# Splitting the last of seven rounds into two in a six-sum graph kernel

## The chip, the cores and the metric

One core of a Trainium2 chip runs the whole program. The metric is the device time of one execution in microseconds (us). The kernel before was timed three times: median 6155.66 us, from 6149.27 to 6156.11.

## The reference, cut to what matters

Four graph blocks work on 6250 nodes with 128 features and 100,000 edges whose destinations are sorted. Each block's result is added to its input and layer-normalised.

```python
edge_index = jnp.stack([src, dst])
x = _layernorm(x + _L0_gnn_ref(x, edge_index, ...))   # attention, 8 heads, then selu
x = _layernorm(x + _L1_gnn_ref(x, edge_index, ...))   # three times: x + segment_sum(x[src], dst), two dense layers
x = _layernorm(x + _L2_gnn_ref(x, edge_index, ...))   # attention, 4 heads, plus a skip product, its own norm
x = _layernorm(x + _L3_gnn_ref(x, edge_index, edge_weight, ...))  # three times: x @ W, weighted segment_sum, bias
```

The second and the fourth block each hold three sums over edges: these are the six sums of the title.

## The kernel before, in words

**Sums as matrix products.** The nodes are cut into 49 tiles of 128. The edges are scattered into two dense adjacency planes in device memory, one of edge counts (fp16) and one of edge weights (fp32). A sum over edges is then a dense product of the node rows with the plane. It is done in rounds of destination tiles, `ROUNDS = (7, 7, 7, 7, 7, 7, 7)` (L46). A round has 49 steps, one for each source tile: a strip of the plane (128 source nodes by 896 destination columns, and 128 extra columns in round 0) is brought by SyncE's DMA queue, and TensorE multiplies the source rows by it in one piece of 512 columns and one of 384, accumulating in two PSUM banks. After the 49 steps a small product (`fix`, L1050) adds a correction, the banks are drained, and the dense layers of the round (the "net") are run in pieces, one piece after every fifth step of the next round (L1133, and L1672 for the other engines). A round's tiles are cut into quads of at most four tiles (`quads_of`, L898), so a round has one quad of four and one of three.

**Three count sums** (`CountSums`, L1256; the order of work of each engine is written out in `count_layers`, L1693). The first ("alone") multiplies bf16 row parts with fp16 strips directly. Its rounds wait until GpSimd has scattered the cells that they read (`s_epoch`, L1361). The second ("wide", 256 features) needs, for each step: the fp16 strip widened to fp32r ("laid", L1426) into one of four strip buffers; a high part of the source rows made by ScalarE (`make_high`, L1437) and a low part made by VectorE (`make_low`, L1445), in a ring of two; then 8 matmuls of TensorE. `make_high` of step n waits for the matmuls of step n-2. The third has its high and low parts at hand, needs only the laid strip, and has 4 matmuls a step. ScalarE lays all strips of the second sum and four of five of the third; VectorE lays the fifth (`by_vector`, L1269). A strip lands in one of five landing places (`LANDING`, L57), and SyncE issues the next DMA for a place once its last strip is laid (L1366).

**What runs beside them.** VectorE computes the weights of the cells of the second plane (`Count.weigh`, L797; one instruction of 8 to 784 columns for each of 784 cell columns), each of which GpSimd then scatters. How many are computed at a step of the sums is planned by `due_by` (L678): two shares for each step of the second sum and one for each step of the third, so that all are done at 85% of all shares. From the second round of the third sum on, the rows of the round before are normalised and the head of attention 2 is made for every full quad of finished tiles (`beside`, L1612). The quads that are left after the last round (`BESIDE`, L49: quads 10, 11 and 12) are made at the end. GpSimd scatters 4 numbers of each of their tiles (L1920), one instruction a tile, and begins attention 2's gathers (L471).

**Three plane sums** (`PlaneSums`, L914; `plane_layers`, L1808) come after attention 2. They read fp32 strips in seven slots, with no laying, and wait in step n for the strip alone. At the end the last round's quads are drained, multiplied, normalised and stored one after the other (L1852 to L1855, L1218).

Between two sums, the first step of the next waits until the last banks of the one before are drained (L1003, L1397). In the wide sum, whose rounds share their banks, so does every round (L1394).

Of the kernel before, what the change touches and what calls it, by code (L numbers as in the profile page):

```python
# [21 lines left out]
TILES = -(-N // P)  # L22
# [10 lines left out]
QUAD = 4  # L33
# [9 lines left out]
assert COLS % NARROW == 0  # L43
SCAN = {NARROW: 12}
ENDING = {NARROW: (12, 7, 4)}
ROUNDS = (7, 7, 7, 7, 7, 7, 7)  # L46
assert sum(ROUNDS) == TILES
SETTLED = sum(ROUNDS[:-1])
BESIDE = SETTLED // QUAD  # L49
SPAN = P + NPAD  # L50
FOLLOWS = 800.0
ROW_BITS = 13
# [1 line left out]
assert SPAN + COLS + 32 <= 1 << ROW_BITS and SPAN % WIPE == 0  # L54
SLOTS, SLOT = 7, P + max(ROUNDS) * P
NEAR = 9 * SLOT
LANDING = 5  # L57
AHEAD = 3
STRIPS = 4
LEAD = STRIPS - 1  # L60
# [6 lines left out]
LANES = 8  # L67
# [4 lines left out]
BATCH = 7  # L72
# [4 lines left out]
RING = 13  # L77
# [53 lines left out]
class Memory:  # L131

    def __init__(self, nc, ctx):
# [23 lines left out]
        gb_at = next_address(nc)  # L157
# [25 lines left out]
        behind, apart = NEAR, TILES * HID - WIDE  # L183
# [21 lines left out]

        self.identity = sb("identity", [P, P])

        strips_at = gb_at + 2 * LANDING * SLOT
        ring_at = strips_at + 4 * STRIPS * SLOT
        assert ring_at + 4 * PARTS * HID <= gb_at + 4 * SLOTS * SLOT and PARTS * HID <= WIPE  # L210
        halves = TILES * D // 2
# [6 lines left out]
        behind = TILES * 152  # L218
        self.first_rooms = [self.gb[:, behind + k * WIDE // 2:behind + (k + 1) * WIDE // 2].bitcast(bf16) for k in range(4)]
        behind += 2 * WIDE  # L220
        self.first_products = self.gb[:, behind:behind + LANES * BATCH]
        assert behind + LANES * BATCH <= NEAR and RING * SLOT // 2 <= SLOTS * SLOT
        self.high = nc.alloc_sbuf_tensor_at("high", [P, TILES, D], fp32r, offset=x_at)
        self.low_part = nc.alloc_sbuf_tensor_at("low_part", [P, TILES, D], fp32r, offset=tmp_at)
        self.strips = nc.alloc_sbuf_tensor_at("strips", [P, STRIPS, SLOT], fp32r, offset=strips_at)
# [23 lines left out]
        n = 8 * (NARROW + 1) + 1  # L249
# [168 lines left out]

    def settled(self, tiles):
        a, b = tiles[0], tiles[-1] + 1  # L420
        if b > SETTLED:
            return self.x[:, a:b, :]
        at = TILES * 140
        return self.big[:, at + a * D:at + b * D].rearrange("p (t d) -> p t d", d=D)

    def kept_rows(self, tiles):
        a, b = tiles[0], tiles[-1] + 1
        if b <= SETTLED:
            return self.settled(tiles)
        flat = self.hidden2[:, :, :].rearrange("p a c -> p (a c)")  # L430
        return flat[:, (a - SETTLED) * D:(b - SETTLED) * D].rearrange("p (t d) -> p t d", d=D)

# [465 lines left out]
def quads_of(r):  # L898

    before = sum(-(-size // QUAD) for size in ROUNDS[:r])  # L900
    a, b = sum(ROUNDS[:r]), sum(ROUNDS[:r + 1])
    return [(before + i, i, range(t, min(t + QUAD, b))) for i, t in enumerate(range(a, b, QUAD))]
# [6 lines left out]

STEPS = len(ROUNDS) * TILES  # L910
NETS = quads_by(len(ROUNDS) - 1)
# [344 lines left out]
class CountSums(PlaneSums):  # L1256
# [11 lines left out]

    def by_vector(self, n):  # L1269

        return not self.wide and self.alone is None and n % 5 == 2

    def laid_by_vector(self, n):
# [21 lines left out]
        return 3 * k + i if self.wide else 3 * (r % 2) + i  # L1295

    def landing(self, n):
        at = (self.first_step + n) % LANDING * SLOT // 2
        return self.m.gb[:, at:at + SLOT // 2].bitcast(fp16)

    def strip(self, n):
# [44 lines left out]
    def sp(self, sp):  # L1346
# [8 lines left out]
        for n in range(STEPS):  # L1355
# [11 lines left out]
            if self.again is not None and (r, s) == (0, 20):  # L1367
                sp.wait_ge(m.s_sum.sem, self.at(m.s_sum, 0))
                m.s_again.up(sp.dma_start(m.kept_rows(range(SETTLED)), by_tile(m.kept)[:, 0:SETTLED, :]), 16)
            if self.again is not None and (r, s) == (1, 20):  # L1370
                sp.wait_ge(m.s_product.sem, self.at(m.s_product, 0))
                m.s_again_last.up(sp.dma_start(m.kept_rows(range(SETTLED, TILES)), by_tile(m.kept)[:, SETTLED:TILES, :]), 16)
            if self.again is not None and r >= 2 and s == 20:
# [319 lines left out]
def count_layers(selu, head, *layers):  # L1693
# [8 lines left out]
    with nc.Block(no_gpsimd_drain=True) as block:  # L1702
# [8 lines left out]
        def _(dve):  # L1711
# [32 lines left out]
            sums.normalize_rows(dve, last)  # L1744
            for g in range(BESIDE, QUADS):
                head.take(dve, g)

        @block.scalar
        def _(act):
# [27 lines left out]
            sums.root(act, last)  # L1777
            for g in range(BESIDE, QUADS):
                head.copy_turned(act, g)
# [5 lines left out]
        def _(pe):  # L1785
# [5 lines left out]
            layers[-1][0].last_net(pe)  # L1791
            head.turn(pe, BESIDE)
            for g in range(BESIDE, QUADS):
                if g + 1 < QUADS:
# [159 lines left out]
class HeadBeside(HeadPart):  # L1954
# [15 lines left out]
    def bank(self, g):  # L1970
        return 2 if g < BESIDE else 5

# [1255 lines left out]
```

How the kernel before makes its waits and increments, by code:

```python
    def up(self, instruction, by=1):  # L101
        instruction.then_inc(self.sem, by)
        self.count += by
# [18 lines left out]
    def wait(self):  # L122
        self.engine.wait_ge(self.done.sem, self.done.count)
# [338 lines left out]
def pass_gathers(m, pool, table, columns, width, row, begin, end):  # L462
    nc = m.nc
    for b, (first, size) in enumerate(plan(columns)):
        if b >= BUFS and begin <= first < end:
            stored = m.s_run_stored[b % BUFS]
            pool.wait_ge(stored.sem, stored.at(16 * (b // BUFS)))
        for r in range(max(first, begin), min(first + size, end)):
            j = r - first
            m.s_rows[b % BUFS].up(nc.gpsimd.indirect_dma_start(
                m.batch(b, columns, row)[:, j, 0:width], None, table,
                bass.IndirectOffsetOnAxis(ap=m.src[:, r:r + 1], axis=0)), 16)
# [2 lines left out]
def fix_gather(m, pool, runs, width, columns):  # L476
    batches = len(plan(columns))
    for b in range(BUFS):
        stored = m.s_run_stored[b]
        pool.wait_ge(stored.sem, stored.at(16 * len(range(batches)[b::BUFS])))
    m.s_fix_row.up(m.nc.gpsimd.indirect_dma_start(
        m.fix[:, 0:width], None, runs, bass.IndirectOffsetOnAxis(ap=m.first_end[:, :], axis=0)), 16)
# [2 lines left out]
def end_gathers(m, pool, runs, width):  # L486
    nc = m.nc
    pool.wait_ge(m.s_fix_stored.sem, m.s_fix_stored.at(16))
    ends = m.ends(width)
    for t in range(TILES):
        m.s_end[t // QUAD].up(nc.gpsimd.indirect_dma_start(
            ends[:, t, :], None, runs, bass.IndirectOffsetOnAxis(ap=m.end_row[:, t:t + 1], axis=0)), 16)
```

## Time and profile before

| | us |
|---|---|
| median of 3 runs | 6155.66 |
| the profiled execution | 6158.55 |
| its span, first to last instruction | 6156.7 |
| TensorE / VectorE / GpSimd / ScalarE busy | 3507.0 / 2954.0 / 3308.0 / 1732.6 |
| mean granted TensorE clock | 0.776 |

The stages, from the timeline: attention 1 and preparation until 1704 us, first count sum 1704 to 2301, second 2307 to 3030, third 3033 to 3405, attention 2 until its tail at about 4437, plane sums 4465 to 6143, end 6156.7. No engine is busy over 57% of the whole, so shares of the whole say little; the stages have to be read one by one.

### The profile page before, as it was taken

The numbers are of one execution on the slowest core, as the hardware profiler recorded it, in microseconds if no ns is written. First come the engines' busy times: TensorE is split into PE (matmuls) and PEld (weight loads), VectorE is DVE, ScalarE is ACT, GpSimd is POOL, SyncE is SP. The second block draws the span as 40 slices with busy tenths as digits, with TensorE's granted clock in tenths as the row PEclk, the third lists the DMA queues.
The fourth block names the chain that finished last, engine by engine and source line by source line (L and its number), as shares of the span: only waits on it lengthen the run. The fifth ranks groups of instructions, "written<-read, shape, count | busy, mean of one in ns | idle before, by whom it ended". The sixth has DMA issues, their size and how long they took to land. (4 is left out here: it accounts for less than half of the span.)

```text
span 6156.7 us, 45427 instructions
## 1 busy us (share of the span) xinstructions
PE 3507.0 (57%) x13778; PEld 2221.4 (36%) x13778; DVE 2954.0 (48%) x6586; ACT 1732.6 (28%) x2167; POOL 3308.0 (54%) x3349
## 2 busy tenths in 40 slices
PE   3000000050099779999999211111099999999999
PEld 2000000010055338888788200010055555555554
DVE  4766666669656664666564455555560000000111
ACT  2443343121011005666677333333240000000000
POOL 5777777577777777777775677777610000000000
PEclk7555555565599889999999555555599999999999
DMA  5566665399954443444577343333378888888887
GB/s 147 191 221 218 210 223 200 102 366 367 338 176 131 122 119 105 121 117 121 148 229 236 103 122 111 112 120 111 126 218 293 296 296 291 296 296 291 302 302 266
DMA packets 551335, 1255.80 MB, mean 204 GB/s; under 512 B 119278, under 2 KB 281684, under 8 KB 542388
## 3 DMA queue, kind: packets, MB, share of 16 engines
q1 hardware_dynamic: 430116, 1126.46, 53.8%
q0 software_dynamic: 119952, 125.65, 8.5%
q8 instruction: 111, 1.82, 0.1%
q14 instruction: 132, 1.08, 0.1%
q10 hardware_dynamic: 1024, 0.79, 0.1%
HBM read 873.83 MB, written 378.71 MB: 203 GB/s over the span
## 5 line engine op out<-in xcount | busy, mean ns | idle before, releaser
L839 POOL DMA_INDIRECT plane<-total,cell x1568 | 1619.7, 1033 | 490.6 <-issue 426.5
L471 POOL DMA_INDIRECT gb<-rows,src x1564 | 1486.4, 950 | 525.5 <-issue 474.9
L1016 PE MATMUL psum<-gb,big 128*128 128x512 f32 (+1 forms) x4116 | 1586.3, 540 | 3.5 <-DVE gb L1040 1.6
L1016 PEld LDWEIGHTS psum<-gb,big 128*128 128x128 f32 x4116 | 769.2, 191 | 719.7 <-issue 503.8
L1415 PE MATMUL psum<-gb,row_part 128*128 128x512 f16 (+1 forms) x2058 | 417.9, 357 | 464.5 <-DMA gb<-plane 464.5
L2489 ACT COPY gb<-turned 128x1632 f32<-128x1632 f32 (+3 forms) x138 | 450.8, 3267 | 722.3 <-DVE turned L2584 722.3
L1415 PE MATMUL psum<-strips,ring 128*128 128x512 f32 (+1 forms) x2744 | 609.8, 376 | 14.9 <-issue 8.5
L2510 PE MATMUL psum<-identity,end_top 128*8 128x128 f32 (+1 forms) x2 | 0.7, 372 | 1083.6 <-DVE end_top L2590 1083.6
L1435 ACT CAST strips<-gb 128x896 fp32r<-128x896 f16 (+1 forms) x617 | 572.9, 947 | 131.2 <-DMA gb<-plane 49.2
L2878 PE MATMUL psum<-w_L_gnn_skip_W,turned 128*128 128x128 f32 x98 | 39.0, 501 | 846.8 <-ACT turned L2896 846.8
L1415 PEld LDWEIGHTS psum<-strips,ring 128*128 128x128 f32 x2744 | 485.8, 189 | 86.7 <-issue 23.7
L2584 DVE TENSOR_TENSOR_SCAN turned<-gb,psum 128x1632 f32<-128x1632 f32 (+3 forms) x138 | 457.8, 3317 | 68.2 <-ACT gb L2471 65.7
L2573 DVE TENSOR_TENSOR psum<-gb,psum 128x1632 f32<-128x1632 f32 (+3 forms) x138 | 444.5, 3221 | 2.3
L753 DVE SCALAR_TENSOR_TENSOR big<-big,passing,psum 128x784 bf16<-128x784 f32 (+10 forms) x455 | 323.7, 781 | 209.2 <-DMA plane<-total,cell 209.0
L1415 PEld LDWEIGHTS psum<-gb,row_part 128*128 128x128 bf16 x2058 | 190.7, 99 | 630.0 <-issue 394.8
L2510 PEld LDWEIGHTS psum<-identity,end_top 128*8 128x8 f32 (+1 forms) x2 | 0.2, 82 | 1084.0 <-DVE end_top L2590 1084.0
L1171 ACT ACTIVATE turned<-turned,c_L_gnn_b 128x512 f32<-128x512 f32 (+1 forms) x42 | 25.8, 661 | 1229.4 <-DVE turned L1200 1229.4
L2878 PEld LDWEIGHTS psum<-w_L_gnn_skip_W,turned 128*128 128x128 f32 x98 | 24.5, 310 | 860.0 <-ACT turned L2896 851.9
L2546 DVE COPY passing<-passing 128x8 f32<-128x8 f32 (+1 forms) x70 | 13.0, 185 | 613.5 <-DMA gb<-rows,src 613.5
L1200 DVE TENSOR_TENSOR turned<-psum,big 128x512 f32<-128x512 f32 (+1 forms) x42 | 24.3, 620 | 549.0 <-PE psum L1057 544.9
L1450 DVE SCALAR_TENSOR_TENSOR ring<-big,ring 128x256 fp32r<-128x256 f32 x343 | 146.3, 426 | 289.5 <-ACT ring L1443 288.4
L1040 DVE TENSOR_TENSOR gb<-gb,identity 128x128 f32<-128x128 f32 x147 | 42.1, 291 | 452.6 <-DMA gb<-plane 452.5
(420 smaller groups left out, 4748.1 us busy)
## 6 DMA issues: line engine op xcount, KB each, us to landing
gb<-plane SPq DMA_DIRECT2D x882, 448.0 KB, 4.1
gb<-plane SPq DMA_DIRECT2D x882, 224.0 KB, 2.9
plane<-turned SPq DMA_DIRECT2D x49, 3200.0 KB, 28.3
plane<-turned SPq DMA_DIRECT2D x49, 1600.0 KB, 10.9
gb<-plane SPq DMA_DIRECT2D x147, 512.0 KB, 4.6
runs<-gb SPq DMA_DIRECT2D x33, 1748.0 KB, 6.2
runs<-gb SPq DMA_DIRECT2D x33, 1610.0 KB, 5.7
gb<-plane SPq DMA_DIRECT2D x147, 256.0 KB, 3.2
```

The lines of the kernel that those rows point to most:

```text
L471: m.s_rows[b % BUFS].up(nc.gpsimd.indirect_dma_start(m.batch(b, columns, row)[:, j, 0:width], None, table, bass.IndirectOffsetOnAxis(ap=m. ...
L753: self.up(("product", k), m.nc.vector.scalar_tensor_tensor(self.rooms[k][:, 0:size], m.keys[g][:, 0:size], m.own_keys[:, own:own + 1], sel ...
L839: done.up(m.nc.gpsimd.indirect_dma_start(plane, bass.IndirectOffsetOnAxis(ap=m.cell[:, r:r + 1], axis=0), total[:, r:r + 1], None), 16)
L1016: mm = nc.tensor.matmul(m.psum[:, self.bank(r, 0, i), 0:nodes], rows, slot[:, a:a + nodes], start=(s == 0), stop=False)
L1040: m.s_own.up(m.nc.vector.tensor_tensor(cells, cells.bitcast(fp32), m.identity[:, :], ALU.add))
L1415: mm = nc.tensor.matmul(m.psum[:, self.bank(r, k, i), 0:nodes], rows, strip[:, a:a + nodes], start=begin, stop=False)
L1435: m.s_strip_act.up(nc.scalar.copy(out, landed))
L1450: m.s_low.up(m.nc.vector.scalar_tensor_tensor(self.ring(n)[:, 1, :], self.source(n % TILES), 0.0, high, ALU.max, ALU.subtract))
L2489: m.s_laid.up(nc.scalar.copy(m.batch(b, B, W)[:, j0:j1, 0:S].rearrange("p j w -> p w j"), summed(n)))
L2573: c.link(nc.vector.tensor_tensor(fed(n).rearrange("p (h c) j -> p h c j", h=H), rows[:, j0:j1, 0:S].rearrange("p j (h c) -> p h c j", h=H) ...
L2584: m.s_summed.up(nc.vector.tensor_tensor_scan(m_turn[:, 0:size_n], scan_mask[:, 0:size_n], fed_flat[:, 0:size_n], 0.0, ALU.mult, ALU.add))
L2878: nc.tensor.matmul(out[:, n, :], self.turned[:, n * P:(n + 1) * P], self.skip[:, 0, :], start=True, stop=False)
```

## The change

The last round of seven tiles becomes a round of four and a round of three. Hence there are 392 steps in a sum instead of 343, and the last two rounds have one quad each: the number of quads, of matmuls and of columns stays, while strips, laid strips, high parts and low parts become more. In rounds of at most four tiles VectorE lays two of five strips, in the wide sum too. There are seven landing places, the two new ones in memory that was free. Tiles 42 to 45 are now kept in another buffer until the end of the third sum, and quad 10 of attention 2's head is made beside the last round, so that quads 11 and 12 are left.

```diff
-ROUNDS = (7, 7, 7, 7, 7, 7, 7)
+ROUNDS = (7, 7, 7, 7, 7, 7, 4, 3)
 assert sum(ROUNDS) == TILES
-SETTLED = sum(ROUNDS[:-1])
-BESIDE = SETTLED // QUAD
+SETTLED = sum(ROUNDS[:-2])
+BESIDE = sum(ROUNDS[:-1]) // QUAD
...
-LANDING = 5
+LANDING, LANDING_NEAR = 7, 5
...
     def settled(self, tiles):
         a, b = tiles[0], tiles[-1] + 1
-        if b > SETTLED:
+        if a >= sum(ROUNDS[:-1]):
             return self.x[:, a:b, :]
+        if a >= SETTLED:
+            return self.kept_rows(tiles)
...
     def by_vector(self, n):
 
+        if self.alone is None and ROUNDS[n // TILES] <= QUAD:
+            return n % 5 in (2, 4)
         return not self.wide and self.alone is None and n % 5 == 2
...
     def landing(self, n):
-        at = (self.first_step + n) % LANDING * SLOT // 2
+        k = (self.first_step + n) % LANDING
+        at = k * SLOT // 2 if k < LANDING_NEAR else (SLOTS + 1) * SLOT + (k - LANDING_NEAR) * SLOT // 2
         return self.m.gb[:, at:at + SLOT // 2].bitcast(fp16)
```

## Rows read from the trace of the kernel before

**Rows 1.** The page: span, and busy us (share) x instructions.

```profile
span 6156.7 us, 45427 instructions
PE 3507.0 (57%) x13778; PEld 2221.4 (36%) x13778; DVE 2954.0 (48%) x6586; ACT 1732.6 (28%) x2167; POOL 3308.0 (54%) x3349
```

**Rows 2.** Timeline of TensorE, first sum's last round: start, us, engine, line [idle before].

```profile
2228.31 7.20 PE L1415 MATMUL psum<-gb,row_part 128*128 128x512 f16 x30 [35.23 <-DMA gb<-plane]
```

**Rows 3.** Windows (length; PE, PEld, DVE, ACT, POOL): wide last, third first, third last.

```profile
2934.10:3030.20 96.10, 96.06 (x453) 80.77 (x454) 52.98 (x189) 65.11 (x104) 74.46 (x72) 1.00 0.44 119
3033.20:3105.70 72.50, 68.25 (x354) 57.24 (x354) 35.26 (x82) 46.05 (x49) 56.55 (x53) 0.98 0.68 203
3357.90:3404.70 46.80, 45.60 (x236) 39.85 (x236) 17.19 (x51) 33.88 (x42) 7.88 (x8) 1.00 0.77 235
```

**Rows 4.** Timeline, wide sum, two steps at TensorE's pace.

```profile
2818.46 0.42 ACT L1443 ACTIVATE ring<-big 128x256 fp32r<-128x256 f32 x1 [0.39 <-PE psum L1415]
...
2818.91 0.42 DVE L1450 SCALAR_TENSOR_TENSOR ring<-big,ring 128x256 fp32r<-128x256 f32 x1 [0.51 <-ACT ring L1443]
...
2820.12 0.42 ACT L1443 ACTIVATE ring<-big 128x256 fp32r<-128x256 f32 x1 [0.40 <-PE psum L1415]
```

**Rows 5.** Timeline, wide sum, a step in which VectorE is late.

```profile
2735.73 0.79 DVE L816 SCALAR_TENSOR_TENSOR passing<-gb,weight 128x552 bf16<-128x552 f32 x1
...
2736.44 0.80 DVE L816 SCALAR_TENSOR_TENSOR passing<-gb,weight 128x560 bf16<-128x560 f32 x1
...
2737.16 0.42 DVE L1450 SCALAR_TENSOR_TENSOR ring<-big,ring 128x256 fp32r<-128x256 f32 x1
...
2737.73 0.47 PE L1415 MATMUL psum<-strips,ring 128*128 128x512 f32 x1 [0.54 <-DVE ring L1450]
```

**Rows 6.** Groups by form, 2934 to 3034 us: busy, mean ns | idle before.

```profile
L1435 ACT CAST strips<-gb 128x896 fp32r<-128x896 f16 x45 | 41.7, 926 | 0.0
L1435 ACT CAST strips<-gb 128x1024 fp32r<-128x1024 f16 x3 | 3.1, 1039 | 2.0 <-PE psum L1415 2.0
L1469 ACT COPY turned<-psum 128x512 f32<-128x512 f32 x2 | 1.1, 582 | 0.0
```

**Rows 7.** Groups by form: VectorE's laying, third sum; its key products, second sum.

```profile
L1433 DVE CAST strips<-gb 128x896 fp32r<-128x896 f16 x59 | 37.9, 643 | 95.3 <-DMA gb<-plane 60.1 <-PE psum L1415 35.1
...
L740 DVE TENSOR_TENSOR passing<-gb,of_lane 128x784 f32<-128x784 f32 x5 | 4.8, 970 | 0.0
```

**Rows 8.** The page's DMA issues: KB each, median us from issue to landing.

```profile
gb<-plane SPq DMA_DIRECT2D x882, 448.0 KB, 4.1
gb<-plane SPq DMA_DIRECT2D x882, 224.0 KB, 2.9
```

**Rows 9.** Waits, third sum's sixth round: us in total, times, longest.

```profile
DVE strips L1433 <- DMA gb<-plane: 20.2, 6, 6.1
ACT strips L1435 <- DMA gb<-plane: 8.7, 11, 2.9
```

**Rows 10.** Timeline from the third sum's end to attention 2.

```profile
3405.15 1.16 ACT L1467 ACTIVATE turned<-psum,c_L_gnn_b2a 128x512 f32<-128x512 f32 x2 [3.56 <-PE psum L1057]
...
3407.11 0.70 DVE L1576 TENSOR_TENSOR psum<-psum,r_L_gnn_b2b 128x512 f32<-128x512 f32 x1 [4.33 <-PE psum L1105]
...
3409.77 0.54 DVE L1576 TENSOR_TENSOR psum<-psum,r_L_gnn_b2b 128x384 f32<-128x384 f32 x1
...
3419.23 0.96 POOL L1920 DMA_INDIRECT spread<-big,spread_row  x1 [19.46 <-DVE big L1916]
...
3430.67 0.98 POOL L2431 DMA_INDIRECT passing<-rows,last_dst  x1 [0.30 <-issue]
```

**Rows 11.** Timeline, end of the kernel.

```profile
6146.28 0.69 DVE L1214 TENSOR_TENSOR x<-psum,x 128x512 f32<-128x512 f32 x1 [1.54 <-PE psum L1105]
...
6150.02 0.55 DVE L1214 TENSOR_TENSOR x<-psum,x 128x384 f32<-128x384 f32 x1
```

**Rows 12.** Windows: the second plane sum's last round.

```profile
5521.00:5596.40 75.40, 75.40 (x213) 38.98 (x212) 6.20 (x15) 1.23 (x2) 0.00 (x0) 1.00 0.89 297
```

More of the change, by code:

```diff
@@ L206, in __init__ @@
         self.identity = sb("identity", [P, P])
-        strips_at = gb_at + 2 * LANDING * SLOT
+        strips_at = gb_at + 2 * LANDING_NEAR * SLOT
         ring_at = strips_at + 4 * STRIPS * SLOT
@@ L221, in __init__ @@
         self.first_products = self.gb[:, behind:behind + LANES * BATCH]
-        assert behind + LANES * BATCH <= NEAR and RING * SLOT // 2 <= SLOTS * SLOT
+        assert behind + LANES * BATCH <= NEAR and (SLOTS + 1) * SLOT + (LANDING - LANDING_NEAR) * SLOT // 2 <= NEAR and RING * SLOT // 2 <= SLOTS * SLOT
         self.high = nc.alloc_sbuf_tensor_at("high", [P, TILES, D], fp32r, offset=x_at)
```

## The prediction, made before the changed kernel was seen

> **What bounds the kernel now.** I read the page first [rows 1]: no engine is busy over 57% of the span, so the stages are read singly. The chain of waits runs along TensorE's matmuls in the sums, and the question at each stage is what starts it and what paces it.
>
> The first sum's last round starts after 35.23 us in which TensorE waited for a strip, and SyncE doesn't ask for that strip before GpSimd has ended its scatter [rows 2]. From 2228.3 us on nothing holds the sums but themselves. At their end GpSimd had been idle 19.46 us when attention 2's head gave it quad 10 [rows 10]; so attention 2 starts as many microseconds later as the sums and their tail take longer. The plane sums are TensorE's alone: 75.40 us busy of 75.4 in a round [rows 12]. So the path is: the sums from 2228 us on, their tail to 3430.67, attention 2, plane sums, end. All four are touched.
>
> **Terms, part by part.** The sum is made against the profiled execution's own 6158.55 us (span 6156.7 and 1.85 around it), which is 2.9 above the median of 6155.66.
>
> *Matmuls.* A short round has half of the matmuls, and the two together have the columns of the old one. In the wide sum a step goes in 1.65 us (ScalarE's high part starts at 2818.46 and again at 2820.12 [rows 4]), 49 steps are 81 us, and the remaining 15 of 96.1 [rows 3] are the net. Split by columns a step of 512 takes 0.94 and one of 384 0.71. In the third sum a full step is half of it, 0.83, and short ones are 0.475 and 0.355. In a plane sum 75.4/49 = 1.54 becomes 0.88 and 0.66. If TensorE stays the pace, nothing is lost or won by this.
>
> *The wide sum's short rounds, where I expect the loss.* Two things there don't halve with the strip.
>
> First the ring. The high part of a step starts when the matmuls two steps back are done; 0.45 later VectorE's low part starts, which takes 0.42 [rows 4], and TensorE starts 0.15 after its end (low part from 2737.16, matmul at 2737.73 [rows 5]). With the 0.2 from the last matmul's issue to ScalarE's start that is 1.22 us behind the matmuls two steps back. It was hidden under a step of 1.65. In a short round two steps take 1.22 and a step of matmuls: (1.22+0.94)/2 = 1.08 and (1.22+0.71)/2 = 0.97 a step.
>
> Second VectorE. Per step it makes a low part (0.45 with its start), and `due_by` gives it 588 cell columns over 85% of 3 x 392 shares, two a step: 1.18 columns a step, be the step long or short. One of 552 columns takes 0.71 to the start of the next [rows 5]. By the plan the seventh round has columns number 542 to 599: 47 of sizes 416 to 784, mean 600, at 0.76, then the key products of a new epoch (two of 0.97 [rows 7]), then 11 small ones of about 0.25. The eighth has numbers 599 to 657, mean size 328, at 0.48. To this come 20 laid strips a round, which VectorE didn't lay in this sum before: 0.64 at 896 columns [rows 7]; for 512 the bounds are 0 and 0.64, I take 0.43, and 0.38 for 384. So VectorE's work is 22+36+2+3+9+3 = 75 us in the seventh and 22+28+8+2 = 60 in the eighth (3 and 2 for own tiles, marks and takes), against 46 and 35 of step matmuls. Rows 5 show that this is a wait and not a matter of averages: with two columns ahead of the low part, the matmul started 0.54 late. During a net piece VectorE runs dry two steps ahead, so of the 15 us of net in the seventh round some 6.5 are added, in the eighth nearly all of its 8.7 but 1.5. In the stretches with small columns the ring's pace holds. I get 80 us for the seventh (TensorE's own floor 61, the plain sum 83) and 63 for the eighth (floor 44).
>
> The drain between rounds of this sum was 3.1 us: products of `fix`, then four copies of 0.58 and less [rows 6]. With one quad it is 2.2 and then 1.9. Together 80+63+4.1 against 96.1+3.1 is **+47.9**. Of this 8.7 is the net of quad 42 to 45, moved out of the third sum's first round (72.5 us [rows 3]), where it stood in TensorE's time: **-8.7**. In the first six rounds VectorE has 1.18 columns a step in place of 1.35; I take **-2** (between 0 and -6, as those rounds are 96 to 98). ScalarE has per short step a high part (0.42) and three of five strips: by 0.88 ns a column between 896 and 1024 [rows 6] a strip of 512 costs 0.59, in all 0.85 with starts, under 0.94 and over 0.71, but under the ring's 0.97.
>
> *The third sum.* All cells are weighed by its fifth round, so the ring and the weighing are out of it. What is left is the strip's way through its place: issue, landing, laying. 448 KB land in 4.1 us, 224 in 2.9 [rows 8]; for 128 and 96 KB the bounds are 0 and 2.9, and the line through the two rows gives 2.4 and 2.2, I take 2.5 and 2.3. With 0.15 and the laying of 0.59 and 0.48 a place turns in 3.24 and 2.93, over seven places 0.46 and 0.42. So the seventh goes at TensorE's 0.48, the eighth at 0.43: 45 us. To it 6.3 us of net and head as before (46.8 less 40.5), 1.6 for quad 10's head, and about 6 (0 to 12) for VectorE's lumps (a join of 2.66, from 3407.11 to 3409.77 [rows 10]) that three steps ahead covered at 0.83 a step and don't at 0.48. That is 59+1 against 47.5: **+11.6** (+1 to +20).
>
> Two more places give 1.66 us more lead in each full round; laying waited for landings 20.2 and 8.7 us in the sixth round [rows 9], most of it hidden by the strips ahead. Taking that each of about four rounds has one delay that the strips ahead don't cover, 1.7 of it back in each is **-7** (0, if all was covered, to -10). Of what is moved here, the store of quads 8 and 9 goes from after the last step into SyncE's queue at step 20 of the eighth round, ahead of strips; it is part of the 6 us of lumps. Quad 10's store stays at the end, and ScalarE's one more copy of kept tiles lies beside attention 2's first gathers: 0.
>
> The Trainium skill, "DMA: Bandwidth & Descriptors", section "Anatomy of one DMA — SWDGE (gpsimd) path", puts a transfer at about 2.0 us fixed and the bytes at 436 GB/s, its fixed part mostly completion. It speaks against halving strips, as do the two rows (half the bytes, 2.9 in place of 4.1); by its figures 128 KB land in 2.3, the eighth round would go at 0.41, and the estimate would fall by 1 us.
>
> *The tail into attention 2.* From 3405.15 to 3419.23 is 14.1 us, then nine scatters at 1.27 to 3430.67 [rows 10]. One copy of 0.58, the join of four tiles (2.66) and two thirds of the normalising fall away, 3.8 in all, and four scatters, 5.1: **-8.9**.
>
> *Plane sums.* At the end a quad of four (6146.28 to 6150.02, 3.7 us [rows 11]) and half a us of its drain go: **-4.2**. At each of two boundaries one drain less: **-1.2**. Strips of 256 and 192 KB have seven slots: 6.2 and 4.6 us for a turn. At 4.1 us to landing [rows 8] the eighth round would just wait (0.69 a step for 0.66); by the smaller strips it doesn't, I take 0 (to +7). The first sum: the same net in all, one more round's end, one smaller drain: 0.
>
> *GpSimd.* It scatters at 1.35 us a column behind the weighing; by the plan it stays behind until the third sum's fourth round, and a few us there hide in its idle time [rows 10].
>
> Sum: 47.9-8.7-2+11.6-7-8.9-4.2-1.2 = +27.5, so 6186.0 in the profiled execution's terms, 6183 in those of the median.
>
> **Rivals.**
>
> *Only the ring binds.* VectorE's 75 and 60 us run beside TensorE's waits. Then 67 and 56 for the short rounds (1.08 and 0.97 a step and most of the net), 20 less: 6163. For it: VectorE was busy 53.0 of 96.1 us in the last wide round [rows 3]. Against it: rows 5.
>
> *Faster: TensorE keeps the pace in all short rounds.* The place is the wide sum's ring: it decides at 0.94 and 0.71 us, if high and low parts are ready that soon. Then short wide rounds are 106 us, +0.2 with drains, net and lighter weighing; the third sum is -5.4, the tails -14.3: -19.5, 6136. Against it: the 1.22 of rows 4 and 5, in which there is little to squeeze.
>
> *Landings don't get shorter.* The wait moves to the strips: 0.52 a step in the third sum's short rounds (+6) and 2.4 in each of three plane sums (+7): 6197, with more stores in the way up to 6206. For it: rows 9; against: rows 8.
>
> **Chances and range.** Forecast 53%, ring only 20%, landings 16%, faster 11%. A change under 0.2% (12.3 us, so 6143 to 6168) can't be told from none. Ring only falls mostly into it, the faster case mostly below, the rest above: faster 12%, same 19%, slower 69%. The forecast's own range is 6172 to 6199; with the ring case and most of the landings case 6150 to 6206.
>
> **What would show it.** Wide sum: short rounds of about 80 and 63 us, VectorE busy over 85% there and TensorE's matmuls released by the low part. Third sum's first round near 64, its short ones near 31 and 28, rounds two to six a little shorter. GpSimd's first gather of attention 2 some 33 us later than 3430.67 [rows 10], end tail 9.4 us in place of 13.6. I am wrong if the wide short rounds take under 120 us together, or if plane rounds of 512 and 384 columns take over 75 together.

## The result and the profile after

The changed kernel took **6194.6 us** (median of 5 runs, 6188.6 to 6198.5). The kernel before, timed alongside, took 6155.7. The ratio is 1.0062 with a 95% interval of 1.0051 to 1.0074, so the change makes the kernel 0.6% slower. The forecast was 6183, its range 6150 to 6206.

The profile page of the kernel after, busy us (compare [rows 1]):

```profile
PE 3519.4 (57%) x13778; PEld 2211.4 (36%) x13778; DVE 2993.2 (48%) x6710; ACT 1736.6 (28%) x2249; POOL 3315.5 (54%) x3349
```

The span grew by 36.1 us to 6192.8, TensorE's busy time only by 12. To see where, both traces are cut at the first and last matmul of each sum, and TensorE's rounds are compared. In both traces the last seven tiles of the first sum begin at 2228.3 us; up to there nothing differs that matters. The first round of a sum is measured without its last piece of 128 extra columns. A gap is the time between two rounds or sums in which no step matmul runs.

| part of TensorE's path | before | after | difference | forecast |
|---|---|---|---|---|
| first sum's last seven tiles and the gap to the wide sum | 78.6 | 90.3 | +11.6 | 0 |
| wide sum, first round | 120.0 | 111.6 | -8.3 | (in the line above) |
| wide sum, rounds two to six with their gaps | 504.1 | 501.6 | -2.5 | -2 |
| wide sum, short rounds (80.88 and 61.72) with gaps to the third sum | 102.2 | 149.8 | +47.6 | +47.9 |
| third sum, first round | 72.4 | 60.5 | -12.0 | -8.7 |
| third sum, rounds two to six | 246.6 | 229.9 | -16.7 | -7 |
| third sum, short rounds (30.63 and 29.54) | 47.4 | 61.1 | +13.7 | +11.6 |
| third sum's end to attention 2's first gather | 26.0 | 17.2 | -8.8 | -8.9 |
| from there to the first plane sum | 1034.7 | 1034.2 | -0.5 | 0 |
| three plane sums | 1677.7 | 1694.0 | +16.3 | -1.2 |
| last matmul of a sum to the end | 13.6 | 9.3 | -4.3 | -4.2 |

The lines add up to +36. Three of them carry the difference to the forecast of +27.5: the plane sums (+17.5 worse), the third sum's full rounds (-13 with its first round, better) and the first boundary (+3).

Windows of the kernel after: the wide sum's two short rounds, the third sum's first, its two short ones (columns as in [rows 3]):

```profile
2934.70:3015.70 81.00, 70.13 (x258) 44.86 (x259) 65.79 (x188) 40.77 (x88) 63.63 (x58) 0.98 0.32 83
3017.70:3079.50 61.80, 52.10 (x230) 37.27 (x231) 50.84 (x182) 35.45 (x81) 48.08 (x46) 1.00 0.36 97
3081.60:3142.20 60.60, 58.05 (x322) 51.10 (x322) 33.45 (x74) 42.88 (x45) 47.80 (x43) 1.00 0.81 247
3377.50:3408.30 30.80, 28.95 (x140) 22.35 (x139) 17.79 (x57) 19.15 (x34) 6.81 (x7) 1.00 0.70 200
3408.50:3438.10 29.60, 23.79 (x121) 21.09 (x119) 12.30 (x41) 15.06 (x31) 4.84 (x5) 0.88 0.64 173
```

In the wide short rounds VectorE, the fourth figure, is busy 65.8 of 81.0 and 50.8 of 61.8 us. Before it was 53.0 of 96.1 for all seven tiles [rows 3]. TensorE has gaps: 70.1 of 81.0 and 52.1 of 61.8.

How such a gap comes about shows in the timeline of the kernel after, in the eighth round:

```profile
3042.37 0.41 DVE L1455 SCALAR_TENSOR_TENSOR ring<-big,ring 128x256 fp32r<-128x256 f32 x1
3042.70 0.35 DVE L1438 CAST strips<-gb 128x384 fp32r<-128x384 f16 x1
3042.97 0.46 DVE L818 SCALAR_TENSOR_TENSOR passing<-gb,weight 128x240 bf16<-128x240 f32 x1
...
3043.36 0.47 DVE L818 SCALAR_TENSOR_TENSOR passing<-gb,weight 128x248 bf16<-128x248 f32 x1
...
3043.76 0.42 DVE L1455 SCALAR_TENSOR_TENSOR ring<-big,ring 128x256 fp32r<-128x256 f32 x1
...
3044.32 1.69 PE L1420 MATMUL psum<-strips,ring 128*128 128x384 f32 x8 [0.44 <-DVE ring L1455]
```

Between two low parts (L1455) stand a laid strip and two weighed columns, so that 1.39 us pass from one low part to the next. The matmuls of a step need some 0.7. The matmul starts 0.14 after the second low part's end, as in [rows 5].

The third sum's end and the way into attention 2, timeline of the kernel after (compare [rows 10]):

```profile
3448.90 0.97 POOL L1925 DMA_INDIRECT spread<-big,spread_row  x1 [12.41 <-DVE big L1921]
...
3455.26 0.98 POOL L2436 DMA_INDIRECT passing<-rows,last_dst  x1 [0.31 <-issue]
```

The join of four tiles (2.66 us before) is gone, five scatters are left of nine, and GpSimd still waits, 12.41 in place of 19.46. Its first gather comes 24.6 us later than before, where 33 were forecast.

The third sum's eighth round hides one long pause. Timeline of the kernel after:

```profile
3416.23 0.93 SPq L1935 DMA_DIRECT2D rows<-big  x2
...
3421.96 0.51 ACT L1440 CAST strips<-gb 128x384 fp32r<-128x384 f16 x1 [4.11 <-DMA gb<-plane]
...
3422.53 0.69 PE L1420 MATMUL psum<-strips,high 128*128 128x384 f32 x1 [3.63 <-ACT strips L1440]
```

and the window behind it (the figure after the counts, 0.50, is the share of TensorE's clock that was granted, here 1.2 of 2.4 GHz):

```profile
3422.50:3425.90 3.40, 3.37 (x11) 3.28 (x12) 2.00 (x8) 1.78 (x5) 0.00 (x0) 0.50 0.53 155
```

SyncE had issued two stores for attention 2's head just ahead of the strip that came late. TensorE stood still for 3.63 us, and its matmuls of 384 columns then started every 0.32 us in place of 0.17 until 3427.4. This pause, of 3.3 to 3.9 us, stands in experiments 1, 2, 4 and 11 too. That the stores caused it is likely by their place, and no run moved them.

### The profile page after: what moved, and what is told of

It reads as the page before. It is cut to its first block and busy times, and to the rows that moved or that the text cites. A ratio compares the mean times of both kernels' runs of the same rounds, so it can differ in the third digit from the quotient of the medians.

```text
span 6192.8 us, 46084 instructions
## 1 busy us (share of the span) xinstructions
PE 3519.4 (57%) x13778; PEld 2211.4 (36%) x13778; DVE 2993.2 (48%) x6710; ACT 1736.6 (28%) x2249; POOL 3315.5 (54%) x3349
## 5 line engine op out<-in xcount | busy, mean ns | idle before, releaser
L1018 PE MATMUL psum<-gb,big 128*128 128x384 f32 (+1 forms) x4116 | 1592.5, 541 | 13.1 <-DVE turned L1202 11.6
L1420 PE MATMUL psum<-gb,row_part 128*128 128x384 f16 (+1 forms) x2058 | 419.8, 358 | 466.4 <-DMA gb<-plane 466.4
L1420 PE MATMUL psum<-strips,ring 128*128 128x512 f32 (+1 forms) x2744 | 626.4, 379 | 39.4 <-DVE ring L1455 18.5
L1440 ACT CAST strips<-gb 128x896 fp32r<-128x896 f16 (+3 forms) x647 | 555.7, 877 | 112.6 <-PE psum L1420 58.6
L1455 DVE SCALAR_TENSOR_TENSOR ring<-big,ring 128x256 fp32r<-128x256 f32 x392 | 167.0, 426 | 294.9 <-ACT ring L1448 291.1
L1202 DVE TENSOR_TENSOR turned<-psum,big 128x512 f32<-128x512 f32 (+1 forms) x42 | 24.5, 620 | 561.2 <-PE psum L1059 557.1
L1042 DVE TENSOR_TENSOR gb<-gb,identity 128x128 f32<-128x128 f32 x147 | 41.9, 291 | 459.3 <-DMA gb<-plane 459.3
```

What stands on the lines that cost most here:

```text
L1018: mm = nc.tensor.matmul(m.psum[:, self.bank(r, 0, i), 0:nodes], rows, slot[:, a:a + nodes], start=(s == 0), stop=False)
L1420: mm = nc.tensor.matmul(m.psum[:, self.bank(r, k, i), 0:nodes], rows, strip[:, a:a + nodes], start=begin, stop=False)
L1440: m.s_strip_act.up(nc.scalar.copy(out, landed))
L1455: m.s_low.up(m.nc.vector.scalar_tensor_tensor(self.ring(n)[:, 1, :], self.source(n % TILES), 0.0, high, ALU.max, ALU.subtract))
```

## A boundary that nobody had priced

The plane sums' full rounds are as before (75.39 each), the short ones take 43.8 and 33.5. What is new stands between the sums: 5.94 and 6.32 us without a matmul, where there were 2.23 and 2.37. The timeline of the kernel after at the first of these:

```profile
5075.24 0.34 PE L1059 MATMUL psum<-spot,fix_low 128*128 128x384 f32 x1
5075.92 0.29 DVE L1042 TENSOR_TENSOR gb<-gb,identity 128x128 f32<-128x128 f32 x1 [1.72 <-DMA gb<-plane]
5077.60 0.29 DVE L1042 TENSOR_TENSOR gb<-gb,identity 128x128 f32<-128x128 f32 x1 [1.38 <-DMA gb<-plane]
5078.89 0.29 DVE L1042 TENSOR_TENSOR gb<-gb,identity 128x128 f32<-128x128 f32 x1 [1.00 <-DMA gb<-plane]
5080.16 0.29 DVE L1042 TENSOR_TENSOR gb<-gb,identity 128x128 f32<-128x128 f32 x1 [0.98 <-DMA gb<-plane]
5080.36 0.55 DVE L1202 TENSOR_TENSOR turned<-psum,big 128x384 f32<-128x384 f32 x1
...
5081.17 1.19 PE L1018 MATMUL psum<-gb,big 128*128 128x512 f32 x1 [5.59 <-DVE turned L1202]
```

TensorE waits for the drain L1202. The drain waits for nothing of its own: TensorE's last product is done at 5075.6. But VectorE's queue has four instructions ahead of it that add the own cells (L1042) to the next sum's first strips, and each waits for a strip of 512 KB to land. These land every 1.27 to 1.29 us. The timeline of the kernel before at the same place:

```profile
5050.37 0.33 PE L1057 MATMUL psum<-spot,fix_low 128*128 128x384 f32 x1
5050.52 0.29 DVE L1040 TENSOR_TENSOR gb<-gb,identity 128x128 f32<-128x128 f32 x1 [0.97 <-DMA gb<-plane]
5050.72 1.15 DVE L1200 TENSOR_TENSOR turned<-psum,big 128x512 f32<-128x512 f32 x2
```

There one own cell stood in the way and its strip landed in time, since strips were asked for once in 1.54 us, which is longer than a landing every 1.28. In a short round the slots come free every 0.66 us, the strips still land every 1.28, and the seven strips ahead are no longer there when the round ends.

The pause costs more than its own length. Windows of the kernel after behind its two boundaries, then of the kernel before behind its first:

```profile
5081.20:5086.20 5.00, 5.00 (x8) 2.55 (x9) 1.86 (x4) 0.36 (x1) 0.00 (x0) 0.50 0.44 154
5635.40:5639.20 3.80, 3.80 (x7) 2.16 (x8) 1.83 (x4) 0.34 (x1) 0.00 (x0) 0.50 0.39 158
5052.20:5057.20 5.00, 5.00 (x17) 2.77 (x18) 1.72 (x4) 0.47 (x1) 0.00 (x0) 1.00 0.64 216
```

After 5.94 and 6.32 us without a matmul the granted clock stands at 0.50 for the first 5.1 and 3.9 us of the next sum; after 2.23 us it stayed at 1.00. Half speed over these stretches loses 2.6 and 2.0 us.

The first boundary has the same form on another engine. Timeline of the kernel after, first sum to wide sum:

```profile
2310.67 7.63 SPq L1381 DMA_DIRECT2D gb<-plane  x11
...
2313.44 1.99 ACT L1440 CAST strips<-gb 128x1024 fp32r<-128x1024 f16 x2 [20.66 <-DMA gb<-plane]
...
2317.86 0.47 ACT L1474 COPY turned<-psum 128x384 f32<-128x384 f32 x1
2318.58 1.08 PE L1420 MATMUL psum<-strips,ring 128*128 128x512 f32 x2 [6.59 <-ACT turned L1474]
```

Here ScalarE's drain (L1474) stands behind the laying of the wide sum's first strips. It did so before too; new is that the first strip is asked for only at 2310.67 and laid from 2313.44 on, 2.2 us after TensorE's last step of the first sum (2311.24). In the kernel before it had landed, and its laying began 0.15 us after the last step (2301.18):

```profile
2301.33 1.99 ACT L1435 CAST strips<-gb 128x1024 fp32r<-128x1024 f16 x2 [33.39 <-PE psum L1421]
```

A start 2.05 us later, less 0.48 for the smaller drain (0.47 for 0.95), is the 1.6 by which this gap grew, from 5.76 to 7.34.

## Experiments

Ratios are to the kernel before, timed alongside on the same chip, with their 95% intervals. It took 6152.6 us beside experiments 1 to 4, 7094.5 beside 5 to 8 and 6150.0 beside 9 to 12, on three different chips, so times are compared across these groups by their distance to it. "Short rounds" are the wide sum's seventh and eighth.

**1. No weighing in the wide short rounds.** The changed kernel, with the plan of the weighing moved:

```diff
-    passed, all_units = 2 * min(p + 1 - STEPS, STEPS) + max(0, p + 1 - 2 * STEPS), 3 * STEPS
-    return min(WIDE, 2 * EACH + (WIDE - 2 * EACH) * passed * 100 // (SHARE * all_units))
+    wide, third = min(p + 1 - STEPS, TILES * (len(ROUNDS) - 2)), max(0, p + 1 - 2 * STEPS)
+    return min(WIDE, 2 * EACH + 3 * wide // 2 + 68 * third // 100)
```

> The changed kernel, but no cell column is weighed in the wide sum's two short rounds: 1.5 columns a step in its six full rounds, none in the short ones, 0.68 a step in the third sum. Theory (VectorE's weighing binds the short rounds, 80.9 and 61.7 us): they fall to the ring's pace, about 67 and 56, so 18 to 20 us less, 6175 against 6194.6; the full rounds grow by up to 4 where columns are large. Rival (the ring of two alone binds, VectorE's work lies beside it): short rounds within 3 us of 80.9 and 61.7, total near 6195.

Measured: 6187.3, ratio 1.0057 (1.0042 to 1.0073); short rounds 68.7 and 57.1. Windows of this kernel in them:

```profile
2945.70:3014.40 68.70, 66.18 (x257) 43.55 (x258) 29.85 (x74) 40.72 (x87) 52.55 (x54) 1.00 0.32 86
3016.50:3073.60 57.10, 49.26 (x230) 37.37 (x231) 27.26 (x73) 34.72 (x81) 43.78 (x43) 1.00 0.38 103
```

The wait (us in total, times, longest) in the eighth round:

```profile
PE psum L1420 <- DVE ring L1455: 7.7, 22, 0.4
```

The weighing cost these rounds 12.2 and 4.7 us; VectorE's 20 laid strips a round are still there. Up to 1.7 of the 12.2 is clock: in the changed kernel it stood at 0.50 from 3007.6 to 3011.0, after a wait of 2.21 us for a low part, and here it stays at 1.00. The work came back elsewhere: with 1.5 columns a step the full wide rounds went from 98.3/96.0/96.9/96.7/96.2 to 100.8/99.6/97.0/96.1/100.5, +10. So the kernel is 34.6 us above the kernel before where the changed one was 38.9; the intervals overlap, and the 18 to 20 us expected didn't come.

**2. The same, with a ring of three steps** (a third high and low part, in memory that `turned` grows by):

```diff
-        return self.m.ring[n % 2]
+        return self.m.ring[n % 3]
...
-        self.wait_used(act, n - 2)
+        self.wait_used(act, n - 3)
```

> As e1_weigh_moved, and the ring of high and low parts has three places, so that a high part waits for the matmuls three steps back. Theory (the ring is what is left once the weighing is gone): short rounds fall further, from about 67 and 56 to 62 and 47, within 3 us of TensorE's own 61 and 44, some 14 us less than e1, total 6162. Rival (what is left is ScalarE's work or the strips' landing): short rounds as in e1, within 2 us.

Measured: 6162.2, ratio 1.0017 (1.0008 to 1.0026); short rounds 61.5 and 49.1. Windows of this kernel:

```profile
2931.70:2993.20 61.50, 61.50 (x257) 44.92 (x258) 28.89 (x75) 39.88 (x88) 47.16 (x48) 1.00 0.36 96
2995.30:3044.40 49.10, 47.27 (x229) 38.09 (x230) 26.57 (x73) 33.87 (x81) 37.82 (x38) 1.00 0.43 118
```

In the seventh round TensorE is busy all of 61.5 us, which is the floor of 61 of the forecast. So of the 80.9 us, 12.2 went with the weighing, another 7.2 with the ring of two, and the rest is TensorE's. In the eighth it is 4.7 and 8.0; 49.1 stays above the 44 estimated. The two shares hold in this order; no run has the ring of three with the weighing left in the short rounds. The full rounds too are shorter than in the first experiment (97.6/96.9/95.9/95.9/97.5).

**3. Seven landing places alone**, on the kernel before, with its seven rounds:

```diff
-LANDING = 5
+LANDING, LANDING_NEAR = 7, 5
...
-        at = (self.first_step + n) % LANDING * SLOT // 2
+        k = (self.first_step + n) % LANDING
+        at = k * SLOT // 2 if k < LANDING_NEAR else (SLOTS + 1) * SLOT + (k - LANDING_NEAR) * SLOT // 2
```

> The kernel before with seven landing places in place of five and nothing else: seven rounds of seven. Theory (the third sum's rounds 1 to 5 fell from 246.6 to 229.8 us in the changed kernel because of the two more places): they fall by 13 to 17 here too, round 0 by 2 to 4, total 6138 to 6143. Rival (they fell because VectorE weighs 0.59 columns a step there in place of 0.67): rounds 1 to 5 within 4 us of 246.6, total 6152 to 6156.

Measured: 6130.5, ratio 0.9966 (0.9952 to 0.9979). The third sum's rounds: 66.4, then 45.4/46.6/50.1/44.9/44.3, then 44.9, in all 23 us less than before. Rounds two to six fell by 15.4, as the theory had it, and not by under 4, as the rival had it; the first fell by 6.0 in place of 2 to 4, and the whole by more than expected. Waits of this kernel in the third sum from its second round on:

```profile
DVE strips L1434 <- DMA gb<-plane: 10.9, 4, 5.5
...
ACT strips L1436 <- DMA gb<-plane: 5.2, 6, 1.6
```

Its sixth round, the weight load's wait for laid strips:

```profile
PEld psum L1416 <- ACT strips L1436: 0.6, 2, 0.4
```

The kernel before in the same stretch of the third sum:

```profile
DVE strips L1433 <- DMA gb<-plane: 60.1, 21, 6.1
...
ACT strips L1435 <- DMA gb<-plane: 40.4, 47, 4.1
```

The kernel before in the sixth round:

```profile
PEld psum L1415 <- ACT strips L1435: 4.5, 4, 2.5
PE psum L1415 <- ACT strips L1435: 3.2, 3, 2.1
```

Laying waited 100.5 us for landings and waits 16.1 now. The forecast took one late strip in each of four rounds. There were 68 in six rounds, and ten with seven places. In the sixth round the weight load's wait for ScalarE's strips fell from 4.5 to 0.6, and the matmuls' own wait of 3.2 is gone (the two overlap and aren't added). Part of the gain is clock: in the third sum it stood at 0.50 for 17.1 us in the kernel before, behind such waits, and for 3.4 in this one. Half speed over the difference is at most 6.8 of the 23 us.

**4. The drain first.** The changed kernel; VectorE makes a plane sum's last drain before it adds the own cells to the next sum's first seven strips:

```diff
-                    if ahead.is_own(r1 * TILES + s1) and not (ahead is first and r1 == 0):
+                    if ahead.is_own(r1 * TILES + s1) and not r1 == 0:
...
                     scale(sums.after, last)
+                    for n in range(ROUNDS[0]):
+                        sums.add_own(dve, n)
```

> The changed kernel, but at each of the two boundaries between plane sums VectorE drains the last quad of the sum before, and only then adds the own cells of the next sum's first strips. Theory (the gap grew from 2.2 to 5.9 and from 2.4 to 6.3 us because the drain stands in VectorE's queue behind four additions, each of which waits for a 512 KB strip): gaps fall to 2 to 3.5 us, total 6 us less, 6188 to 6190. Rival (TensorE would wait for the landing of the next sum's strips anyway): gap plus first round stay within 2 us of 93.8 and 93.5, total near 6194.

Measured: 6178.9, ratio 1.0045 (1.0029 to 1.0060). Timeline of this kernel at the first plane boundary:

```profile
5070.89 0.56 DVE L1202 TENSOR_TENSOR turned<-psum,big 128x384 f32<-128x384 f32 x1 [1.42 <-PE psum L1059]
...
5072.48 1.74 PE L1018 MATMUL psum<-gb,big 128*128 128x512 f32 x4 [1.63 <-DVE gb L1042]
```

The gaps are 1.98 and 1.62 for 5.94 and 6.32, and the first rounds behind them 85.29 for 87.83 and 87.22: 13.1 us together, and the kernel is 26.3 above the kernel before in place of 38.9. The two gaps give 8.7 of this. The other 4.5 are the clock: with pauses of under 2 us it stays at 1.00 behind both, and 2.6 and 2.0 were lost to half speed in the changed kernel. The window behind the first:

```profile
5072.50:5077.50 5.00, 5.00 (x16) 2.78 (x17) 1.06 (x4) 0.00 (x0) 0.00 (x0) 1.00 1.02 412
```

The strips land no sooner, but TensorE takes 1.74 for a step of the first round, and strips that land every 1.28 keep up with it. The theory priced the gaps alone and so expected 6; the rival is refuted.

**5 to 8. Four runs that tell little.** They were timed on a chip where the kernel before took 7094.5 us (median of 35), some 940 more than elsewhere: the first count sum's first three rounds took 210 to 350 us each in place of 67 to 72, with TensorE waiting for strips, which are asked for once GpSimd has scattered their cells (373.0 us for one strip with the planes split). What slowed that part isn't known; the runs on other chips don't show it. Their wide and third sums, whose weighing came at other times, can't be compared with the other traces; the plane sums can. All four were repeated below.

> The changed kernel, but VectorE lays no strips in the wide sum; ScalarE lays them all there. Theory (VectorE binds the short wide rounds, and its 20 layings a round are 9 and 8 us of that): rounds of 80.9 and 61.7 us fall to 73 to 76 and 57 to 60. ScalarE then has a high part and a laying in each step, 1.1 us, under the 1.53 of VectorE in the seventh round, but about the ring's pace in the eighth; total 5 to 10 us less than 6194.6. Rival (ScalarE becomes the bound): the seventh within 2 us of 80.9, the eighth longer than 61.7, total not less than 6194.

> The kernel before, with the last round split in the three plane sums alone; the count sums keep seven rounds and five landing places. Theory (the plane part of the change costs 2.2 us in each sum's short rounds, 3.7 to 4 in each of two gaps, 1.5 in each of two first rounds, and gives 4.3 back at the end): gaps of about 6, end tail 9.3, total 12 us more than before, 6163 to 6167. Rival (the plane part pays by its shorter tail and drain, as the prediction had it): 6146 to 6150.

> Seven rounds of seven, seven landing places and a ring of three high and low parts. Theory (full wide rounds are at TensorE's pace of about 96 us but for the steps in which VectorE is late, and a third place hides these): rounds of 96.9, 96.9, 97.9 and 97.9 fall to about 96 and drains from 3.11 to 2.91, 5 to 8 us less than e3_landing7_alone, 6123 to 6126. Rival (a late low part is late whatever the ring holds): within 2 us of 6130.5.

> Seven rounds of seven and seven landing places in the count sums; the last round split in the plane sums alone, with the drain ahead of the next sum's own cells. Theory (with the order mended the split costs 2.2 us in each of three sums and gives 0.9 back in two first rounds and 4.3 at the end): total within 2 us of e3_landing7_alone's 6130.5. Rival (the shorter tail is a gain of its own once the order is mended): 6124 to 6127.

Measured: no laying by VectorE 1.0043 (1.0025 to 1.0061), short rounds 83.6 and 79.3; planes split alone 1.0003 (0.9983 to 1.0023), gaps 6.36 and 5.92; landing places and ring 0.9971 (0.9950 to 0.9993); landing places, planes split and drain first 0.9988 (0.9967 to 1.0008), gaps 1.26 and 2.13. The gaps are within 0.9 us of those in experiments 12 and 10.

**9. Seven landing places and the ring of three** on the kernel before, both edits as above.

> The kernel before with seven landing places in the third sum and a ring of three steps in the wide one; rounds 7x7. Its wide rounds are paced by TensorE (96 us with the net, 1.66 a step), so a deeper ring should add little: theory: the third sum as in the run with the landing places alone (-22 in the span or so), the wide rounds 0 to -3 in all, time 6125 to 6135 against 6155. Rival (the ring of two also costs in full rounds whenever VectorE has two columns in a row): wide rounds 1 to 2 us shorter each, 6115 to 6122.

Measured: **6124.2**, ratio 0.9956 (0.9942 to 0.9970), the lowest of all. Its interval overlaps that of experiment 3, so the times alone don't separate the two. Window of this kernel in its wide sum, the sixth round:

```profile
2828.90:2924.90 96.00, 95.93 (x453) 80.77 (x454) 68.42 (x191) 66.79 (x107) 74.78 (x70) 1.00 0.44 114
```

Every wide round but the first takes 95.9 us now; two had 98 before. By the traces the wide sum is 8.5 us shorter than in experiment 3, more than the 0 to 3 expected. The rounds that took 96.8 and more are 0.9 to 2.0 shorter, the two at TensorE's pace no more than 0.1: that is the rival's mechanism, where VectorE is late, though the rival's time of 6115 to 6122 wasn't reached.

**10. Landing places, plane sums split, drain first**, on the kernel before; the count sums keep seven rounds:

```diff
+        ROUNDS = (7, 7, 7, 7, 7, 7, 4, 3)
+        STEPS, NETS = len(ROUNDS) * TILES, quads_by(len(ROUNDS) - 1)
         tail = SkipTail(m, own4, 4, lng, G[0], low)
```

> The kernel before with seven landing places, the last round split in the plane sums alone, and the drain of a plane sum ahead of the next sum's own cells. Theory (what costs at the two boundaries is the drain behind four own cells that wait for 512 KB strips): against the landing places alone -4.2 at the end, gaps of about 2 in place of 6 and a first round of 85.3 in place of 87, +2.2 for each split round: together -3 to +2, so 6128 to 6133 against 6155. Rival (the split itself costs in the plane sums, by strips that land late): gaps short, but short rounds of over 78.5 together, time 6136 or more.

Measured: 6132.7, ratio 0.9969 (0.9957 to 0.9982). Gaps 1.25 and 1.25, first rounds 85.29, short rounds 43.8 and 33.9 to 34.9. By the trace the plane sums are 3.6 longer than in the kernel before (the short rounds +9.0, the boundaries and the rounds behind them -3.9, the first round -1.6) and the end 4.3 shorter. The short rounds grew by 3.0 a sum, more than the 2.2 of the theory. Split plane sums buy nothing, even with the drain first: 17.3 us under the kernel before, against 22.1 with the landing places alone, with intervals that overlap.

**11. No strip laid by VectorE in the wide sum**, on the changed kernel:

```diff
-            return n % 5 in (2, 4)
+            return n % 5 in (() if self.wide else (2, 4))
```

> The changed kernel, in which VectorE lays no strip in the wide sum's two short rounds (ScalarE lays all five of five). By the theory that VectorE's sum of work sets the pace there, 11 and 8 us of laying leave it: short rounds of 80.9 and 61.7 become 70 to 75 and 55 to 59. But ScalarE then has a high part (0.42) and a strip (0.59 to 0.70) in each step, 1.05 to 1.15 us: its 49 steps are 51 to 56 and the net's copies. Rival (ScalarE becomes the bound in the eighth round, where steps of 1.26 leave it little): the seventh falls by 5 to 8, the eighth by nothing or grows, time 6185 to 6192.

Measured: 6186.0, ratio 1.0056 (1.0042 to 1.0069), an interval that overlaps the changed kernel's own; short rounds 77.6 and 59.5. Windows of this kernel in them:

```profile
2937.80:3015.50 77.70, 69.67 (x258) 44.78 (x259) 59.42 (x169) 50.39 (x107) 60.62 (x57) 0.98 0.33 87
3017.50:3077.10 59.60, 51.86 (x230) 37.34 (x231) 46.09 (x164) 42.20 (x99) 46.22 (x44) 1.00 0.37 101
```

The weight load's wait for laid strips in the seventh:

```profile
PEld psum L1420 <- ACT strips L1440: 16.1, 25, 2.2
```

And in the eighth:

```profile
PEld psum L1420 <- ACT strips L1440: 15.8, 31, 1.0
```

In the changed kernel these waits were 9.1 and 5.2 us. VectorE's busy time fell by 6.4 and 4.7 us, not by the 11 and 8 expected, and the rounds by 3.3 and 2.2: ScalarE was near the pace too, and part of the gain went into waits for its strips. Neither theory's numbers were met in full; the seventh round lost less than the rival's 5.

**12. The last round split in the plane sums alone**, on the kernel before.

> The kernel before, the last round split in the three plane sums alone. Theory: +2.2 for each split round (+6.6), the two gaps 2.3 to 6 and the first rounds behind them 86.2 to 87.5 (+10), the end -4.3: +12, so 6165 to 6170 against 6155. Rival (the gaps come from what the sums before left behind, not from the split): gaps of 2.3, +2.3, 6158.

Measured: 6163.4, ratio 1.0021 (1.0012 to 1.0030). Timeline of this kernel at its first plane boundary:

```profile
5047.47 1.19 PE L1016 MATMUL psum<-gb,big 128*128 128x512 f32 x1 [5.76 <-DVE turned L1200]
```

Gaps 6.10 and 6.19 (+7.7), first rounds 87.9 and 87.0 (+2.6, again with the clock at 0.50 for their first 5.3 and 3.5 us), short rounds +2.4, +2.5 and +3.2, the first plane sum's first round -0.5, the end -4.3: +13.5, and +13.4 timed. The rival is refuted: the plane part of the loss is the split's own.

## Why the prediction was nearly right, and where it wasn't

*What bounds it.* Right. All of the loss lies on TensorE's path from 2228 us on; what ran beside it (GpSimd, ScalarE's copies) changed the time by 0.5 us in attention 2. The forecast didn't have the clock: every pause of TensorE was priced at its length.

*The wide sum's short rounds.* Right in size and in its two causes: 80 and 63 us were forecast, 80.9 and 61.7 measured. Experiment 1 took the weighing out and gave 68.7 and 57.1, against the 67 and 56 of the ring's own pace; experiment 2 took the ring out too and left TensorE's floor in the seventh round. How 80 and 63 follow from VectorE's 75 and 60 us was a judgement more than a sum: 75 and 6.5 of net are 81.5, not the 83 that the text calls the plain sum. One sign was set too high: VectorE is busy 81 and 82% there, not over 85. It is late by its order (two columns and a strip between two low parts), and idle in other steps.

*Rounds two to six of the wide sum, the moved net, the tail, the end.* -2, -8.7, -8.9 and -4.2 were forecast. The first, third and fourth are -2.5, -8.8 and -4.3. Of the -2.5 of rounds two to six, 1.0 is the gap after the first round (5.05 for 6.07, where the kernel before had the clock at 0.50), so that 1.5 at most is left for the lighter weighing. The second is mixed with the landing places' share; -12.0 is what both gave in that round. Experiment 3 has 6.0 for the places alone, which leaves 6.0 for the net, if the two add up, where 8.7 were forecast.

*The third sum's short rounds.* 60 forecast with quad 10's head, 61.1 measured. The sum in the prediction is off by 0.9: 59+1 against 47.5 is 12.5, where it has 11.6; the table has 13.7. And the eighth round came out near its number by another way. A step in 0.43 us, as a place turns, isn't in the trace: between waits a step took 0.35, TensorE's own pace. The time went into waits of 1.69 and 3.63 us and into 4.9 us of matmuls at half clock, about 2.4 lost. The forecast had such lumps, stores ahead of strips among them, at 6 us for both rounds, but not what the clock adds. Landings do get shorter with their size, which the third rival denied. The DMA issues of the kernel after:

```profile
gb<-plane SPq DMA_DIRECT2D x147, 128.0 KB, 2.3
gb<-plane SPq DMA_DIRECT2D x147, 96.0 KB, 2.0
```

The line through [rows 8] gave 2.4 and 2.2, and 2.5 and 2.3 were taken. The Trainium skill, "DMA: Bandwidth & Descriptors", section "Anatomy of one DMA — SWDGE (gpsimd) path", states 2.0 us fixed and the bytes at 436 GB/s for transfers that GpSimd issues; an estimate by it is 2.3 and 2.2. On SyncE's queue 2.3 and 2.0 were measured, so here it was nearer than the values taken.

*Landing places.* The mechanism held, the size didn't: -7 was the term, "each of about four rounds has one delay that the strips ahead don't cover". In the changed kernel the full rounds two to six gave 16.7; alone, in experiment 3, the places gave 15.4 there and 23 in the whole third sum. The bound of -10 was broken too. The row that should have told it is the wait of ScalarE and VectorE over all rounds (100.5 us, 68 times), not that of one round.

*Plane sums: the step that failed.* "At each of two boundaries one drain less: -1.2", and slots at 0. The plane sums alone changed by +16.3. Of this 10.3 are the two boundaries and the rounds behind them, shown by experiments 4 and 12: the drain is queued behind own cells that wait for the next sum's strips. The forecast counted the drain's own time and never asked what stands ahead of it on VectorE, nor what a pause of 6 us does to the clock. The gaps grew by 7.7 and half clock took 4.5, while 0.9 of net (eight matmuls, quad 42 to 45) left each of the two rounds. The short rounds add 6.9. That is about the +7 that was kept as the upper end for the slots, but by luck: 2.7 of it is the same net, which now runs in the three eighth rounds, 0.9 is one more gap a sum, and at most 3.3 are left for strips that came late. Waits of the kernel after in the first plane sum's eighth round:

```profile
PEld psum L1018 <- DMA gb<-plane: 4.4, 13, 0.7
```

Its own test in the prediction said so: over 75 us for the two short rounds would show it wrong, and they took 77.0 to 77.9. (The round of seven took 75.4 itself, so this sign would have shown without any loss.)

*The first boundary.* 0 was forecast, as the same net in all. Net moved from the wide sum's first round into the first sum's last one, as expected; +3.3 is left. The gap, 7.34 for 5.76, is 1.6 of it, by the first strip that lands late; the other 1.7 aren't explained. No run put ScalarE's drain first there.

*Cancelling errors.* The forecast missed by +17.5 in the plane sums, by -13 in the third sum's full rounds, by +3.3 at the first boundary and by +2.1 in the third sum's short rounds. That the total came out 8.6 us off (+36.1 for +27.5) owes something to luck.

*What beats both.* The part of the change that pays is the landing places, 0.9966 alone. With the ring of three on the kernel's seven rounds it is 0.9956, by 8.5 us in the wide sum's trace and within the intervals of the times.

## What to carry to other kernels

Before a round is cut into shorter ones, list what doesn't shrink with it: here the low part, the weighed columns that are planned by the step, the ring's turn, and the landing of the next stage's full-sized strips. The drain here waited in VectorE's queue for everything that the four additions ahead of it waited for; at a boundary put the drain that another engine waits for ahead of work for the next stage. Price a pause of TensorE with the slower matmuls behind it: here 6 us of pause took 2.0 to 2.6 us more. And count how often a prefetch is late over all rounds, since the waits of one round hide how near to the edge it runs.

## What the runs showed that was not expected

What the late drain cost in the next sum's first round was all clock. That round takes 85.3 us with the clock at 1.00 (experiment 4), 87.8 and 87.2 with 0.50 for its first 5.1 and 3.9 us (the changed kernel), 87.9 and 87.0 with 0.50 for 5.3 and 3.5 us (experiment 12): each time the difference is half of the slow stretch, within 0.1 us.

At the end of a short plane round the DMA queue is the limit: strips of 512 KB landed every 1.27 to 1.29 us (5077.60, 5078.89, 5080.16), which is some 410 GB/s, while seven full-sized strips ahead had been enough at one step in 1.54 us.

Two landing places more took away 84 of 100 us in which strips to be laid had not landed. The strips are then asked for two steps sooner, 1.9 us by a round of 45.4 us.
